# Order of work in the merged first stage: the first q and k pair a unit ahead, scores and turns behind chunk blocks

## What is computed

```python
h = _L0_tok_ref(x, w1, b1, w2, b2, pos_emb)          # attention in shifted windows of 4 x 4, 8 heads, output projection
h = h + _L0_attn_ref(_layernorm(h), qkv_w, ...)      # attention of 8 heads over 3136 tokens of an image, relative bias
h = h + _L0_ffn_ref(_layernorm(h), ...)              # the top half of the tokens by a gate through a gelu MLP
```

## Time and profile before

| | us |
|---|---|
| median of three runs | 6252.09 |
| lowest, highest | 6249.62, 6258.36 |
| the profiled execution | 6254.11 |
| its span, first to last instruction | 6252.1 |
| of it, merged first stage (TensorE at work) | about 117 to 1188 |
| TensorE busy over the span | 5853.5 (94%) |

### The profile page before, as it was taken

How to read it: one execution, slowest core, us unless ns; L and a number is a source line. 1 busy time by engine, 2 the same in 40 slices (tenths; PEclk the granted TensorE clock), 3 DMA queues, 4 the chain that set the end, 5 groups by cost and what they waited for, 6 DMA issues and landing times. The chain is left out here.

```text
span 6252.1 us, 121385 instructions
## 1 busy us (share of the span) xinstructions
PE 5853.5 (94%) x37810; PEld 3448.2 (55%) x37810; DVE 4373.6 (70%) x8484; ACT 3276.0 (52%) x6740; POOL 4323.8 (69%) x1447
## 2 busy tenths in 40 slices
PE   1888888699999999999999999999999999986899
PEld 1666666455555555555555555555555555533566
DVE  1666666587777787777777777777777777736540
ACT  0444444246666666666666666666666666641222
POOL 0333333368888888888888888888888888864453
PEclk9999999889999999999999999999999999997999
DMA  2222222411001101101110110110011000014432
GB/s 46 76 92 90 93 88 92 122 32 33 27 25 36 35 16 36 32 27 25 38 40 18 33 41 21 36 33 27 25 36 35 16 17 17 15 55 129 115 93 46
DMA packets 199805, 297.69 MB, mean 48 GB/s; under 512 B 40436, under 2 KB 164614, under 8 KB 196230
## 3 DMA queue, kind: packets, MB, share of 16 engines
q1 hardware_dynamic: 184206, 269.32, 15.2%
q0 software_dynamic: 12432, 19.38, 1.5%
q10 hardware_dynamic: 2664, 2.62, 0.2%
HBM read 166.35 MB, written 124.51 MB: 47 GB/s over the span
## 5 line engine op out<-in xcount | busy, mean ns | idle before, releaser
L1274 DVE TENSOR_REDUCE tops<-ps_m 128x1 f32<-128x448 f32 (+1 forms) x5600 | 3120.0, 617 | 906.6 <-PE ps_m L1177 856.9
L1250 ACT ACTIVATE prob<-ps_s 128x448 f32<-128x448 f32 (+1 forms) x5600 | 2613.3, 548 | 1749.5 <-PE ps_s L1113 1710.4
L1083 POOL TENSOR_TENSOR tile_sum<-prob 128x1792 f32<-128x1792 f32 x448 | 1803.0, 4025 | 658.3 <-ACT prob L1250 658.1
L1113 PE MATMUL ps_s<-queries,keys 97*128 97x448 f32 (+1 forms) x5600 | 2197.3, 397 | 13.7 <-ACT prob L1250 7.6
L1177 PE MATMUL ps_m<-keys,queries 96*128 96x448 f32 (+1 forms) x5600 | 2090.5, 380 | 35.9 <-DMA keys<-k_parts 20.6
L1083 POOL TENSOR_TENSOR tile_sum<-tile_sum,prob 128x1792 f32<-128x1792 f32 x448 | 1807.4, 4034 | 31.8
L1113 PEld LDWEIGHTS ps_s<-queries,keys 97*128 97x128 f32 (+1 forms) x5600 | 1041.6, 187 | 1154.6 <-ACT prob L1250 660.4
L1129 PE MATMUL ps_o<-prob,values 128*32 128x448 f32 x11200 | 1342.0, 551 | 3.0 <-ACT prob L1250 1.2
L1177 PEld LDWEIGHTS ps_m<-keys,queries 96*128 96x128 f32 (+1 forms) x5600 | 1061.6, 190 | 241.9 <-DVE tops L1274 85.6
L324 POOL TENSOR_TENSOR logit<-logit,top 112x896 f32<-112x896 f32 x112 | 194.6, 1738 | 462.1 <-DVE top L581 462.1
L1129 PEld LDWEIGHTS ps_o<-prob,values 128*32 128x32 f32 x11200 | 226.5, 108 | 379.4 <-issue 244.3
(11 more groups left out here) (182 smaller groups left out, 4171.2 us busy)
## 6 DMA issues: line engine op xcount, KB each, us to landing
queries<-q_parts SPq DMA_DIRECT2D x288, 160.0 KB, 3.3
keys<-k_parts SPq DMA_DIRECT2D x96, 392.0 KB, 7.2
xT<-in_x SPq DMA_DIRECT2D x56, 224.0 KB, 3.1
hidden<-h SPq DMA_DIRECT2D x28, 448.0 KB, 3.3
q_parts<-hi SPq DMA_DIRECT2D x56, 224.0 KB, 1.9
q_parts<-lo SPq DMA_DIRECT2D x56, 224.0 KB, 1.9
k_parts<-hi SPq DMA_DIRECT2D x56, 224.0 KB, 1.9
k_parts<-lo SPq DMA_DIRECT2D x56, 224.0 KB, 1.9
```

Source lines behind the costliest of these rows:

```text
L1083: nc.gpsimd.tensor_tensor(tile_sum[k % 2][:, :, :], left, prob[:, t % SLOTS, :, :], ALU.add).then_inc(summed, 1)
L1113: mm = nc.tensor.matmul(o[:, 0:CH], keys[x.u][:, j, at:at + k], queries[x.v][:, j, own:own + CH], start=True, stop=not last, skip_group_ch ...
L1250: nc.scalar.activation(prob[0:k, t % SLOTS, j, :], ps_s[0:k, score_bank(x.hm, i), 0:CH], ACT.Exp).then_inc(exp_done, 1)
L1274: nc.vector.tensor_reduce(tops[0:rows, j, r - blocks[0], c:c + 1], ps_m[0:rows, e % MB, 0:CH], AX.X, ALU.max).then_inc(m_used, 1)
```

## The change

In the orders of all four engines: pair 0 of the odd unit moves from the start of its round to the end of the round before (bank 1), and pair 0 of the even unit from behind `project_2(2)` to behind the odd unit's first scores (bank 0), so each first pair stands a unit ahead of where it stood. Pair 1 keeps about its place. The second scores of both units move behind `project_2(0)` and `project_2(2)`. `project_2(1)` and `project_v2(1)` move from behind the second turn to between the first weigh and the second turn. Banks and waits are set to match; `keep_qk` waits for the scores of the unit before the last only. On VectorE `logits` of the second scores goes behind `high(0)` and `high(2)`, on GpSimd `low(0)` and `low(2)` go ahead of a shift. The arithmetic and the number of instructions stay as they are.

The diff, with lines that stay left out where they say nothing more (GpSimd, TensorE, VectorE, ScalarE in this order):

```diff
--- before.py
+++ after.py
@@ -336,19 +336,21 @@
...
             def one(m, units, norm, project, last=False):
+                if project:
+                    low(m - 2, 0)
                 if units:
                     shift(4 * m + 1, 1)
-                if project:
-                    low(m - 2, 0)
                 if norm:
...
                     shift(4 * m + 2, 0)
+                if project:
+                    low(m - 2, 2)
+                if units:
                     shift(4 * m + 3, 1)
                 if project:
-                    low(m - 2, 2)
                     low(m - 2, 3)
...
@@ -455,29 +457,27 @@
...
 
                 n, before = 2 * m, m - 2
+                if project:
+                    project_2(before, 0, third)
                 if units:
                     scores(n, 0, 1)
-                if project:
-                    project_2(before, 0, third)
-                if units:
                     if project:
                         pe.wait_ge(xT_kept, ONE + CT * before + 1)
                     else:
                         pe.wait_ge(v_kept, ONE + n + 1)
-                    project_qk(n + 1, 1, 0, 0)
+                    project_qk(n + 1, 1, 1, 0)
                 if norm:
                     if project:
                         pe.wait_ge(xT_kept, ONE + CT * before + 2)
+                    else:
+                        pe.wait_ge(qk_kept, ONE + QK * (n + 1) + 2)
                     hidden(m - 1, 0, bank[1])
                 if units:
-                    pe.wait_ge(qk_kept, ONE + QK * (n + 1) + 2)
-                    project_qk(n + 1, 1, 1, 0)
                     if project:
                         pe.wait_ge(full_ready, ONE + QK * before + 1)
                     turn(n, 0)
-                    if norm:
-                        pe.wait_ge(h_kept, ONE + 2 * (m - 1) + 1)
-                    project_v(n + 1, 1, 1)
+                    pe.wait_ge(qk_kept, ONE + QK * (n + 1) + 4)
+                    project_v(n + 1, 1, 0)
                     pe.wait_ge(t_kept, ONE + 2 * n + 1)
                 if norm:
...
@@ -485,19 +485,21 @@
...
                 if units:
                     weigh(n, 0, 0)
+                if project:
+                    if norm:
+                        pe.wait_ge(h_kept, ONE + 2 * (m - 1) + 1)
+                    project_2(before, 1, bank[1])
+                if units:
                     if norm:
                         pe.wait_ge(h_kept, ONE + 2 * (m - 1) + 2)
                     turn(n, 1)
-                if project:
-                    if units:
-                        pe.wait_ge(qk_kept, ONE + QK * (n + 1) + 4)
-                    project_2(before, 1, bank[0])
-                if units:
                     scores(n + 1, 1, 0)
+                    if not last:
+                        pe.wait_ge(v_kept, ONE + n + 2)
+                        project_qk(n + 2, 0, 0, 0)
                     weigh(n, 0, 1)
 
                     n = n + 1
-                    scores(n, 1, 1)
                 if project:
                     if not units:
...
@@ -505,23 +507,27 @@
...
                             pe.wait_ge(full_ready, ONE + QK * before + 1)
                     project_2(before, 2, third)
-                if units and not last:
-                    pe.wait_ge(v_kept, ONE + n + 1)
-                    project_qk(n + 1, 0, 0, 1)
-                if project:
-                    pe.wait_ge(full_ready, ONE + QK * before + 2)
+                if units:
+                    scores(n, 1, 1)
+                    if not last:
+                        if project:
+                            pe.wait_ge(full_ready, ONE + QK * before + 2)
+                        elif norm:
+                            pe.wait_ge(h_kept, ONE + 2 * (m - 1) + 1)
+                        project_qk(n + 1, 0, 1, 1)
+                if project:
+                    if last:
+                        pe.wait_ge(v_kept, ONE + n + 1)
+                    elif units:
+                        pe.wait_ge(qk_kept, ONE + QK * (n + 1) + 2)
                     project_2(before, 3, bank[0])
                 if units:
-                    if not last:
-                        pe.wait_ge(qk_kept, ONE + QK * (n + 1) + 2)
-                        project_qk(n + 1, 0, 1, 1)
                     if project:
                         pe.wait_ge(full_ready, ONE + QK * before + 3)
                     turn(n, 0)
                     if not last:
-                        if project:
-                            pe.wait_ge(full_ready, ONE + QK * before + 4)
-                        project_v(n + 1, 0, 0)
+                        pe.wait_ge(qk_kept, ONE + QK * (n + 1) + 4)
+                        project_v(n + 1, 0, 1)
                     pe.wait_ge(t_kept, ONE + 2 * n + 1)
                 if project:
...
@@ -529,29 +535,25 @@
...
                 if units:
                     weigh(n, 1, 0)
+                if project:
+                    pe.wait_ge(full_ready, ONE + QK * before + 4)
+                    project_v2(before, 1, bank[0])
+                if units:
                     if project:
                         pe.wait_ge(v2_kept, ONE + 2 * before + 1)
                     turn(n, 1)
-                if project:
-                    if units and not last:
-                        pe.wait_ge(qk_kept, ONE + QK * (n + 1) + 4)
-                    elif norm:
-                        pe.wait_ge(h_kept, ONE + 2 * (m - 1) + 1)
-                    project_v2(before, 1, bank[1])
+                    if not last:
+                        scores(n + 1, 0, 0)
+                        pe.wait_ge(v_kept, ONE + n + 2)
+                        project_qk(n + 2, 1, 0, 1)
                 if norm:
-                    if units and not last:
-                        pe.wait_ge(v_kept, ONE + n + 2)
-                    elif project:
-                        pe.wait_ge(full_ready, ONE + QK * before + 4)
-                    turn_xn(m - 1, 0, bank[0])
                     if project:
                         pe.wait_ge(v2_kept, ONE + 2 * before + 2)
-                    else:
-                        pe.wait_ge(qk_kept, ONE + QK * (n + 1) + 4)
+                    turn_xn(m - 1, 0, bank[0])
+                    if units and not last:
+                        pe.wait_ge(qk_kept, ONE + QK * (n + 2) + 2)
                     turn_xn(m - 1, 1, bank[1])
                 if units:
-                    if not last:
-                        scores(n + 1, 0, 0)
                     weigh(n, 1, 1)
 
...
@@ -559,6 +561,7 @@
...
             project_v(0, 0, 0)
             scores(0, 0, 0)
+            project_qk(1, 1, 0, 1)
             rounds(pe, one)
 
...
@@ -648,14 +651,14 @@
...
                 n, before = 2 * m, m - 2
+                if project:
+                    high(before, 0)
                 if units:
                     logits(n, 0, 1)
-                if project:
-                    high(before, 0)
                 if norm:
...
                 if units:
-                    keep_v(n + 1, 1, 1)
+                    keep_v(n + 1, 1, 0)
                 if norm:
...
@@ -669,20 +672,22 @@
...
                     n = n + 1
-                    logits(n, 1, 1)
                 if norm:
...
                     high(before, 2)
+                if units:
+                    logits(n, 1, 1)
+                if project:
                     high(before, 3)
                 if units and not last:
-                    keep_v(n + 1, 0, 0)
+                    keep_v(n + 1, 0, 1)
                 if project:
...
                 if project:
-                    keep_v2(before, 1, bank[1])
+                    keep_v2(before, 1, bank[0])
                 if units:
...
@@ -698,9 +703,11 @@
...
 
+            FIRST_UNIT = 0
+
             def keep_qk(n, u, pair, at):
-                if pair == 0:
-                    act.wait_ge(s_ready, ONE + 2 * (n - u))
+                if pair == 0 and n is not FIRST_UNIT:
+                    act.wait_ge(s_ready, ONE + 2 * (n - 1))
                 act.wait_ge(qk_ready, ONE + 2 * n + pair + 1)
...
@@ -752,15 +759,16 @@
...
                 if units:
-                    keep_qk(n + 1, 1, 0, 0)
                     keep_qk(n + 1, 1, 1, 0)
...
                     keep_sums(n, 0)
+                if project:
+                    keep(before, 1, bank[1])
+                if units:
                     keep_t(n, 1)
-                if project:
-                    keep(before, 1, bank[0])
-                if units:
+                    if not last:
+                        keep_qk(n + 2, 0, 0, 0)
                     keep_sums(n, 1)
...
@@ -768,12 +776,10 @@
...
                 if units and not last:
-                    keep_qk(n + 1, 0, 0, 1)
+                    keep_qk(n + 1, 0, 1, 1)
                 if project:
...
                 if units:
-                    if not last:
-                        keep_qk(n + 1, 0, 1, 1)
                     keep_t(n, 0)
...
```

(10 more changed lines are left out.)

## The result

The changed kernel takes 6167.5 us (median of four runs, 6163.1 to 6169.9); the kernel before took 6250.9 in the runs that belong to these (6245.9 to 6258.4). The ratio is 0.9865, with a 95% interval from 0.9848 to 0.9882: 83 us less. The forecast of 6176 said 76 less.

What follows compares the result with a forecast made beforehand. TensorE bounds the merged first stage; 37.45 - 4.06 + 0.59 + 0.72 = 34.70 us a round, 2.75 less over 25 rounds (69), with edges 74, with clock 76: 6176 us, range 6155 to 6208.

Steps and rivals of the forecast that it cites:

- waits that go: TensorE's five waits per loop round, before second scores, second turns and second turn_xn, all get covered: -4.06 us.
- rival 2: Chain on other engines longer than walked: high(1) and rstd swap, unit n+1's first turn 0.8 us later, 6196; chance 0.19.
- The new wait: Before the second turn_xn, TensorE waits for ScalarE to empty the odd advance pair's bank: +0.59 us a round.
- the boundaries: On TensorE, changes between small tiled matmuls and full blocks, or turn and scores, cost more: +0.72 us a round.
- Rival 1: TensorE's boundary costs are hidden by early weight loads; period 34.37, kernel 6168 us; chance 0.13.
- The cover of 0.17: At T(n+1, 0), unit n+1's first turn: keep(2) allows it 11.85 us after weigh, TensorE arrives at 12.02, no wait.
- high(3) and the shift: VectorE's cast high(3) meets GpSimd's shift(n+1, 1) and takes 0.95 us longer, inside a cover of 1.7.
- The slower rival: VectorE's high(2) delays the odd unit's second softmax over 4.5 us; for example period 38.0, kernel 6266; chance 0.04.
- Rival 4: The covered TensorE waits only move to the next block; period stays at 37.4 us; chance 0.02.
- The edges: Outside the loop: first rounds -4.7 us, last round -0.9, tail +0.4; with the loop's 69, a gain of 74.
- fewer falls: TensorE's clock drops to its lower level less often in the stage: 1 to 2 us gained, making 76.

Runs made afterwards that it cites:

- Numbers 2: Changed kernel with the second scores back ahead of project_2(0) and project_2(2) on TensorE; 6179.0 us beside 6246.8, period 35.00.
- number 4: Kernel before with only the second scores moved behind project_2(0) and project_2(2) on TensorE; 6234.9 us beside 6246.8, period 37.12.
- Number 3: Changed kernel with VectorE's logits ahead of high(0), high(2) and GpSimd's shift ahead of low(0), low(2), as before; 6169.6 us beside 6246.8, period 34.53.
- number 6: Changed kernel with only the even unit's first pair ahead, the odd unit's back at the start of its round; 6158.3 us beside 6265.3, ratio 0.9828.
- number 9: Changed kernel with only the even unit's first pair ahead, measured again on another chip; 6150.0 us beside 6251.8, ratio 0.9835.
- Number 8: Changed kernel unaltered, measured once more; 6173.5 us beside 6251.8, ratio 0.9871.
- number 1: Changed kernel with project_2(1) and project_v2(1) back behind the second turns, ScalarE's keep(1) behind keep_t(n, 1); 6215.8 us beside 6246.8, period 36.12.

## Why the prediction was right, point by point

**The sum in the loop.** Predicted period 34.70, measured 34.53. The term "waits that go", 4.06, came out whole, and T(n+1, 0) had no wait, so rival 2 did not come about. The new wait was put at 0.59 and is shown as 0.49. Of the boundaries, put at 0.72, 0.65 were measured (34.04 - 33.39); 37.45 - 4.06 + 0.49 + 0.65 = 34.53. Rival 1, that the boundaries are hidden, can't be told from the forecast by the time: the 6168 it gave is what was measured, and 34.53 lies midway between its period of 34.37 and the 34.70. It is refuted by what the trace shows: TensorE's busy time rose by 0.65 where rival 1 had it stay at 33.39, the pair after scores is shown for 1.78 and not 1.68, and its wait of 0.39 before T(n+1, 0) isn't there.

**The way the sum was made** hid something. I counted each wait against the block set in front of it. Numbers 2 and 4 show that the odd half's waits don't add up like that: scores' wait and the pair's bank wait are two faces of one chain, weigh to turn, of 14.04 us. That chain was in the text, but only in its new form (11.85 with keep(2) as its end); that it was longer before, through the copy of the even pair, and that the advance of that pair is what cuts it, I had not seen. The sum was right since all parts came together; what each part was credited with (1.67 us for the scores' move, say) was not.

**The cover of 0.17.** It held, but by 0.06: the copy was done 11.78 after weigh and not 11.70, with the 0.15 to TensorE that is 11.93, and the turn came at 11.99 and not at 12.02. Both ends had moved against it, by 0.08 and 0.03, so that it held is in part luck. Rival 2 asked for high(1) and rstd to swap; they did not (714.88 and 714.92, again 0.04 apart). The cost it would have had was not tried.

**high(3) and the shift** did meet, but the cast came first, 0.16 us ahead (last section), and took its short time, as VectorE's busy time of 24.11 against 25.16 shows. The objection I had drawn from the 1.34 us cast had no object here; the extra 0.95 was predicted and did not come. It was under cover either way.

**The slower rival** (3) needed the softmax of the odd half's second scores 4.5 us late. Number 3 shows that the place of logits and high doesn't move the period at all. Rival 4, that the waits move to the next block, is refuted by the waits listed above for the change as a whole. For one part it is what happens: number 4 covers the 1.67 us wait in full, and the time comes back two blocks on. So that a wait is well covered, the ground on which I gave this rival little, does not settle it.

**The edges.** 74 was the sum without the clock, 76 with it. The stage ended 80.6 us earlier (project_v2's last start 1185.97 before, 1105.37 now). It divides so: up to the first block of the loop 5.7 (186.70 to 181.03; predicted 4.7). The 25 rounds 25 x 2.92 = 73.0 (predicted 69), and 3.2 more, since the loop before took 939.35 us (186.70 to 1126.05) and not 25 x 37.45 = 936.25; after, it took 863.16. Those 3.2 are two falls of the clock in the loop of the kernel before, of which I had read one:

```profile
205.33 1.10 PE L392 MATMUL ps_s<-qk 32*112 32x112 f32 x16 [1.67 <-DVE logit L576]
206.37 2.94 PE L439 MATMUL ps_t<-xnT,w_qkv 128*128 128x448 f32 x4
```

The same two blocks take 0.66 and 1.77 in the other rounds, 1.6 less. At 806.14 it happened again (1.10 and 2.91, behind a wait of 1.67; granted clock 0.57 from 806 to 810, as from 205 to 209). In the changed kernel's loop it did not happen. Last round and tails: +1.3 (61.8 before, 63.1 now), where I had forecast -0.5. There the step failed that a wait costs its own length:

```profile
1065.71 1.03 PE L402 MATMUL ps_t<-ident,prob 112*112 112x112 f32 x8 [2.02 <-ACT full L738]
1067.75 3.75 PE L448 MATMUL ps_t<-w_qkv,xnT 128*112 128x256 f32 x8 [1.01 <-ACT probT L726]
1071.43 0.98 PE L413 MATMUL ps_t<-probT,v 112*32 112x112 f32 x16
```

With no pair left to fill it, TensorE waits 2.0 and 1.0 us in a row, and the project_v2 behind them takes 3.75 us, where it took 1.98 in the kernel before (at 1150.87). The granted clock is 0.50, its level of 1.2 GHz, from 1067.7 to 1073. In the profile of number 6 the same block, behind the same two waits, took 1.98, and in that of number 9, the same program, 3.61, so the fall comes in some executions and not in others. Last round and tails took 61.4 in the one and 62.8 in the other: the fall is worth 1.4 of the 1.8 by which the forecast missed here. The 1 to 2 us that I had counted for fewer falls came out as 3.2 less 1.4, which is luck.

**The rest of the 83.** The two profiled executions differ by 91.0 us in span, 10.4 more than the stage does. Number 8 is the same program as the changed kernel and its stage ended at the same place (last project_v2 at 1105.15), yet its span is 6172.2 against 6161.1. From the start of the last project_v2 to the end it took between 5055.7 and 5075.2 over the eleven profiled executions, 5066.1 in that of the kernel before, in no order that follows the edits. So this is how executions and chips differ behind the stage, and no work of the change; of the median's 83 the stage has 81.

## What to carry to other kernels

A wait in the profile is worth its time only if nothing else in the same stretch ends at the same point: before counting it, add up the chain through the other engines from the last common event to the next one, in the old order too. When work is pulled ahead to fill a gap, it occupies a bank that somebody has to empty; put one short block between it and the next user of that bank, or leave it where the gap is already filled. Try each of two symmetric halves of such a change by itself: here one was worth 2.4 us a round and the other, where it was put, cost 0.76.

## What the runs showed that I had not expected

This wait of TensorE costs a little more than the idle time shown: 0.65 for 0.49 (turn_xn in two pieces is 1.57 from start to weigh, in one 0.92). Where the other 0.16 goes, no run shows; the two waits of number 1 cost what they show, 1.59.

A cast on VectorE, 1.34 us when it began in the middle of a shift on GpSimd, took 0.38 when it began 0.16 us before one (cast at 723.24, shift at 723.40); the shift took 1.76 and not 1.68. The kernel before has such a pair too, with the same two times (cast at 717.72, shift at 717.88). By the page "SBUF — State Buffer" of the Trainium skill, in its section on SBUF's two separate sides, the one that starts first gets the shared port pair and the other blocks. The order agrees; but the shift grew by 0.08 us only, beside a cast of which 0.22 lay over it, so no full block of the shift is shown.

```profile
723.24 0.38 DVE L640 CAST hi<-full 128x448 fp32r<-128x448 f32 x1
723.40 1.76 POOL L324 TENSOR_TENSOR logit<-logit,top 112x896 f32<-112x896 f32 x1 [0.88 <-DVE top L584]
```
